# Turning two adjacency tiles per late neighbour product in a graph attention and GraphSAGE kernel

## The chip, the cores and the metric

The kernel runs on one core of a Trainium2 chip. The metric is the device time of one execution in microseconds (us); lower is better. The timed runs shown are three, and one more execution was profiled.

## The reference

16 graphs (the batch) of 1024 nodes with 512 features each and a dense 0/1 adjacency matrix go through two layers. Each layer is followed by a residual and a layer norm over the features:

```python
feats = einsum('bnf,hfu->bhnu', X, W)                    # 8 heads x 64 units
dense = leaky_relu(e_self[..., :, None] + e_neigh[..., None, :], 0.2)
att = softmax(dense + NEG_BIG * (1.0 - A), axis=-1)
x1 = layernorm(x + relu(concat_heads(att @ feats) + b))  # layer 0

agg = (adj @ x1) / max(adj.sum(-1), 1e-6)                # layer 1
out = layernorm(x1 + relu(concat([x1, agg]) @ W1.T))
```

## The kernel before

**Tiles.** A graph's 1024 rows are T = 8 row tiles of 128, and HALF is 4. The adjacency matrix of a graph is loaded in the same 8 row tiles of 512 KB in f32. Each is transposed on TensorE (`turn_adj`: 8 transposes of 128x128 on the bf16 halves of the words into one PSUM bank) and evicted by VectorE into `adj_t` (`adj_rows`: times a constant, written as uint16). The whole `adj_t` of a batch is used by the masks of all 8 heads, by the degree and by the aggregation of layer 1, so it can be overwritten for the next batch only when the aggregation is done.

**Slots and banks.** The raw adjacency tiles have three slots in `adj_nat` (`ADJ_SLOTS`): tile t goes to slot t % 3 and can be loaded when tile t - 3 has been turned. Turned tiles alternate between PSUM banks 3 and 7 (`ADJ_BANKS`), so the turn of tile t waits for the eviction of tile t - 2. Tiles 0 and 1 share their slots with the first four row tiles of the next batch (`lead_x`), tile 2 has its slot to itself. The tiles from 3 on are loaded late, by `load_late_adj`, which first waits for the turn that frees the slot.

**A batch.** On each engine the order of the work is written out by hand in a function `batch(b, more)`; it stands in a hardware loop over batches 0 to 14 and once more, written out, for batch 15. The engines meet only at semaphores. Within a batch TensorE does, in this order: the head (score product of the second half of the rows, features of row tiles 4 and 5, turns of adjacency tiles 6 and 7, features 6 and 7); 8 heads of 8 masked key tiles each (48 small matmuls a key tile); the degree; scores and features of the first half of the next batch; the aggregation; and the tail. The tail loops over row tiles t = 0 to 7: neighbour product, own product of t + 1, turn of x1 tile t + 2. In its second half it also holds turns for the next batch: `turn_adj(b + 1, t - HALF)` and `turn_x(b + 1, t)`. Behind the loop stand the turns of tiles 4 and 5 and two waits for the last row tile's results:

```python
                if more:
                    turn_adj(b + 1, 4)
                    turn_adj(b + 1, 5)
                    pe.wait_ge(o2_sb.sem, o2_sb.at(b, T))
                    pe.wait_ge(o_sum.sem, o_sum.at(b, T))
```

**The other engines in the tail.** For each row tile t ScalarE divides the neighbour product by the degree (`by_degree`, L422 through L414). VectorE's `ln1(t)` adds the two products (L779), adds the residual (L783) and takes the statistics (L786, L789); `ln1_end(t)` normalises (L794, L797) into `y_out`, which has two halves, so that tile t waits until the store of tile t - 2 has landed (`y_stored`). `ln1_end(t - 1)` follows `ln1(t)`. Ahead of the sum, from t = 5 on, `ln1` holds the split of a row tile of the next batch (`x_low`, L600) and one `adj_rows` (L605). In the next batch's head, VectorE's `adj_rows(b, 6)` stands ahead of the values of the first head and `adj_rows(b, 7)` behind them.

**SyncE's queue.** All loads and stores are issued by SyncE from one queue in the order written, with its waits in between. In the tail each t holds: a wait for the residual of tile t, the row load of tile t for the next batch, the store of t - 2, and from t = 4 on one late adjacency load. At the start of a batch's heads it stores the scores, loads the first two score broadcasts, and waits for the turns of tiles 6 and 7 before it loads the leading row tiles of the next batch.

**The prologue** ahead of the loop does for batch 0 what the tail does for the others, with tiles 0 to 5 turned and evicted.

Of the kernel before, what the change touches and what calls it, by code (L numbers as in the profile page):

```python
# [43 lines left out]
def gat_sage_kernel(nc, x, adj, gat_w, gat_b, gat_self, gat_neigh, sage_w, out):  # L44
    B, N, D = x.shape
    H, _, U = gat_w.shape
    T = N // P
    KC = D // P
    HALF = T // 2
# [21 lines left out]
    with ExitStack() as ctx:  # L71
# [180 lines left out]
        def rows(v):  # L252

            return v.rearrange("h u -> (h u)").partition_broadcast(P)
# [4 lines left out]
        def col(c):  # L259
            return slice(c * P, (c + 1) * P)  # L260
# [4 lines left out]
        def stand(engine):  # L265

            engine.sem_inc(turnstile, 1)
# [3 lines left out]
        @block.sync  # L271
        def _(sp):
            for c in range(KC):
                sp.dma_start(w_raw[:, c, :].rearrange("p (h u) -> p h u", h=H),
                             gat_w[:, col(c), :].rearrange("h p u -> p h u")).then_inc(w_in[0], 16)
            for t in range(HALF):
                sp.dma_start(lead_x[:, t, :], x[0, t * P:(t + 1) * P, :]).then_inc(lead_in[t].sem, 16)
            sp.dma_start(a_bc[:, 0, :], rows(gat_self)).then_inc(w_in[1], 16)
            sp.dma_start(a_bc[:, 1, :], rows(gat_neigh)).then_inc(w_in[1], 16)
            sp.dma_start(bias_bc[:, :], rows(gat_b)).then_inc(w_in[2], 16)  # L280
            sp.dma_start(sage_raw, sage_w.rearrange("(c p) f -> p c f", p=P)).then_inc(w_in[3], 16)
            sp.sem_inc(y_stored[0], 16)
            sp.sem_inc(y_stored[1], 16)

            def load_x(b, t):
                sp.dma_start(xs[:, t, :], x[b, t * P:(t + 1) * P, :]).then_inc(x_in[t].sem, 16)

            def load_lead(b, t):
                sp.dma_start(lead_x[:, t, :], x[b, t * P:(t + 1) * P, :]).then_inc(lead_in[t].sem, 16)

            def load_tail(b, t):
                sp.dma_start(tail_x[:, t - HALF, :], x[b, t * P:(t + 1) * P, :]).then_inc(tail_in[t - HALF].sem, 16)

            def load_adj(b, t):
                s = t % ADJ_SLOTS
                sp.dma_start(adj_nat[:, s, :], adj[b, t * P:(t + 1) * P, :]).then_inc(a_in[s].sem, 16)

            def load_late_adj(b, t):
                sp.wait_ge(at_ps.sem, at_ps.at(b, t - ADJ_SLOTS + 1))
                load_adj(b, t)  # L300

            def store_y(b, t):
                sp.wait_ge(y_ok.sem, y_ok.at(b, t + 1))
                sp.dma_start(out[b, t * P:(t + 1) * P, :], y_out[:, t % 2, :]).then_inc(y_stored[t % 2], 16)

            def store_scores(b, i):
                sp.wait_ge(sc_f32.sem, sc_f32.at(b, i + 1))
                half = slice(i * HALF * P, (i + 1) * HALF * P)
                sp.dma_start(s_dram[:, half], sc_row[0:H, half]).then_inc(s_stored.sem, 16)

            def load_scores(b, h):
                if h >= 2:
                    sp.wait_ge(stepped.sem, stepped.at(b, (h - 1) * T))
                sp.dma_start(s_bc[:, h % 2], s_dram[h].partition_broadcast(P)).then_inc(s_in[h % 2].sem, 16)

            def first_scores(b):

                store_scores(b, 1)
                sp.wait_ge(s_stored.sem, s_stored.at(b, 32))
                load_scores(b, 0)  # L320
                load_scores(b, 1)

            load_adj(0, 2)
            for t in range(HALF, T):
                load_tail(0, t)
            sp.wait_ge(w1_ps, 2 * KC)
            for t in range(T):
                load_x(0, t)
            for s in range(2):
                sp.wait_ge(xt_ps.sem, xt_ps.at(0, 2 * s + 2))  # L330
                load_adj(0, s)
            store_scores(0, 0)
            for t in range(3, T):
                load_late_adj(0, t)
            with sp.Fori(0, B - 1) as b:
                first_scores(b)
                for s in range(2):
                    sp.wait_ge(at_ps.sem, at_ps.at(b, T - 1 + s))
                    stand(sp)
                    load_lead(b + 1, 2 * s)  # L340
                    load_lead(b + 1, 2 * s + 1)
                load_adj(b + 1, 2)
                for h in range(2, H):
                    load_scores(b, h)
                    if h in (3, 4):
                        s = h - 3
                        sp.wait_ge(xt_ps.sem, xt_ps.at(b + 1, 2 * s + 2))
                        stand(sp)
                        load_adj(b + 1, s)
                sp.wait_ge(masked.sem, masked.at(b, H * T))  # L350
                stand(sp)
                for t in range(HALF, T):
                    load_tail(b + 1, t)
                store_scores(b + 1, 0)
                for t in range(T):
                    sp.wait_ge(res_ok.sem, res_ok.at(b, t + 1))
                    load_x(b + 1, t)
                    if t >= 2:
                        store_y(b, t - 2)
                    if t >= 4:  # L360
                        load_late_adj(b + 1, t - 1)
                store_y(b, T - 2)
                store_y(b, T - 1)
                load_late_adj(b + 1, T - 1)
            first_scores(B - 1)
            for h in range(2, H):
                load_scores(B - 1, h)
            for t in range(T):
                store_y(B - 1, t)
            for s in range(2):  # L370
                sp.wait_ge(y_stored[s], 16 * (B * T // 2 + 1))
# [161 lines left out]
        def _(dve):  # L533
# [87 lines left out]
            def batch(b, more):  # L621
# [26 lines left out]
                dve.wait_ge(chain.sem, chain.at(b, steps[0]))  # L648
                dve.tensor_scalar(ts_hi[:], ts[:], 0.0, None, ALU.max).then_inc(weights_in.sem, 1)
                feature_rows(b, 5)  # L650
                adj_rows(b, 6)
                for s in range(2):
                    dve.wait_ge(y_stored[s], b * (16 * T // 2) + 16)
                dve.wait_ge(ft_sb.sem, ft_sb.at(b, HALF))
                dve.wait_ge(weights.sem, weights.at(b, 2))
                dve.wait_ge(ones_ok.sem, ones_ok.at(b, 1))
                value_parts(b, 0, FIRST)
                adj_rows(b, 7)
                dve.wait_ge(at_sb.sem, at_sb.at(b, T))


# [106 lines left out]
                def ln1(t):  # L768

                    s = t % 2  # L770
                    if t >= 2:
                        dve.wait_ge(y_ok.sem, y_ok.at(b, t - 1))
                    if more and t == T - 1:
                        ones_column(b + 1)
                    if more and t >= HALF + 1:
                        x_low(b + 1, t - 1)
                        adj_rows(b + 1, t - HALF - 1)
                    dve.wait_ge(o2_sb.sem, o2_sb.at(b, t + 1))
                    dve.tensor_tensor(z[:, s], bank[O1_BANKS[s]][:], o2s[:, s], ALU.add).then_inc(o_sum.sem, 1)  # L779
                    if more and t == T - 1:  # L780
                        x_low(b + 1, T - 1)
                    dve.wait_ge(o_sum.sem, o_sum.at(b, t + 1))
                    dve.scalar_tensor_tensor(out=z[:, s], in0=z[:, s], scalar=0.0, in1=xs[:, t, :],  # L783
                                             op0=ALU.max, op1=ALU.add).then_inc(res_ok.sem, 1)
                    dve.wait_ge(res_ok.sem, res_ok.at(b, t + 1))
                    dve.bn_stats(stats[:, s], z[:, s]).then_inc(chain.sem, tick())  # L786
                    dve.wait_ge(chain.sem, chain.at(b, steps[0]))
                    stand(dve)
                    dve.bn_aggr(mv1[:, s], stats[:, s]).then_inc(ln1_mv.sem, 1)  # L789
# [25 lines left out]
                    if t >= 1:  # L815
                        ln1_end(t - 1)
                if more:
                    adj_rows(b + 1, 3)
                ln1_end(T - 1)
                if more:  # L820
                    adj_rows(b + 1, 4)
                    adj_rows(b + 1, 5)
                assert steps[0] == chain.per_batch, steps

            dve.wait_ge(w_in[2], 16)
# [5 lines left out]
            first_maximum(0)  # L831
            for t in range(HALF, T):
                x_low(0, t)
            for t in range(6):
                adj_rows(0, t)
            with dve.Fori(0, B - 1) as b:
                batch(b, True)
# [3 lines left out]
        def _(pe):  # L841
# [59 lines left out]
            def batch(b, more):  # L901
# [9 lines left out]
                pe.wait_ge(diag_ok.sem, diag_ok.at(b, 1))  # L911
                mm(bank[6][:, 0:SC], ones16[:], diag16[:], True, True).then_inc(max_ps.sem, 1)
                features(b, 5)
                turn_adj(b, 6)
                turn_adj(b, 7)

                def key_tile(h, jt, queries):

# [119 lines left out]
                for t in range(T):  # L1038
# [8 lines left out]
                        own(t + 1)  # L1047
                    if t + 2 < T:
                        turn_x1(t + 2)
                    if more and t >= HALF:  # L1050
                        turn_adj(b + 1, t - HALF)
                    if more and HALF <= t < T - 1:
                        turn_x(b + 1, t)
                    if more and t == T - 2:
                        turn_x(b + 1, T - 1)
                if more:
                    turn_adj(b + 1, 4)
                    turn_adj(b + 1, 5)
                    pe.wait_ge(o2_sb.sem, o2_sb.at(b, T))
                    pe.wait_ge(o_sum.sem, o_sum.at(b, T))  # L1060

# [5 lines left out]
            pe.wait_ge(ft_sb.sem, ft_sb.at(0, 2))  # L1067
            for t in range(HALF, T):
                turn_x(0, t)
            for t in range(6):  # L1070
                turn_adj(0, t)
            with pe.Fori(0, B - 1) as b:
                batch(b, True)
# [23 lines left out]
```

## Time and profile before

| | |
|---|---|
| median of 3 runs | 3609.08 us (3599.88 to 3612.85) |
| profiled execution | 3602.66 us, span 3600.9 us |
| granted TensorE clock, mean | 0.974 |
| TensorE busy | 3413.5 us, 95% of the span |
| VectorE busy | 2467.0 us, 69% |
| ScalarE busy | 1738.2 us, 48% |
| GpSimd busy | 285.0 us, 8% |
| DMA | 248.58 MB, mean 69 GB/s |

The span runs from the first to the last instruction of the program. PE is TensorE, DVE is VectorE, ACT is ScalarE, SP is SyncE. A batch takes about 222 us; the first batch boundary is at about 277 to 300 us of the span. Matmuls overlap, so a duration is longer than the distance to the next start.

### The profile page before, as it was taken

Reading aid. Unit: us, or ns where it says so; the run is one execution under the profiler, and the core shown is the slowest. Engines: PE = TensorE matmul, PEld = TensorE weight load, DVE = VectorE, ACT = ScalarE, POOL = GpSimd, SP = SyncE. Lnnn points to the kernel's source line nnn. Section 1 sums busy time; section 2 is a strip of 40 time slices with the busy share of each in tenths; the row PEclk is TensorE's granted clock in tenths of the full one; section 3 lists DMA queues with packets and bytes.
Section 4 is the critical chain, followed back from the end, with each engine's and each line's share of the span. In section 5 each row is a group of like instructions: output and inputs, shape, how many; then the busy total and the mean of one; then the engine's idle time right before and its main releaser. Section 6 shows DMA issues by size and latency. Waiting matters only on the chain.

```text
span 3600.9 us, 136785 instructions
## 1 busy us (share of the span) xinstructions
PE 3413.5 (95%) x59456; PEld 2912.9 (81%) x59456; DVE 2467.0 (69%) x4364; ACT 1738.2 (48%) x2185; POOL 285.0 (8%) x253
## 2 busy tenths in 40 slices
PE   6998989989899998999989899898998989989998
PEld 5978879787796877969779697886977869788795
DVE  5857668576685756858578485774857758576685
ACT  2635436364363644626346273462735527355363
POOL 0010100101001010100101001010010100101001
PEclk9999999999999999999999999999999999999999
DMA  5113031120312203122031220312203131130310
GB/s 170 59 38 108 26 113 57 51 99 23 116 51 60 96 18 122 45 76 81 20 125 39 77 79 25 125 33 89 68 27 123 33 98 59 38 118 27 94 33 24
DMA packets 98408, 248.58 MB, mean 69 GB/s; under 512 B 14720, under 2 KB 14720, under 8 KB 97792
## 3 DMA queue, kind: packets, MB, share of 16 engines
q1 hardware_dynamic: 97792, 239.38, 20.6%
q8 instruction: 507, 8.31, 1.0%
q14 instruction: 109, 0.89, 0.1%
HBM read 205.26 MB, written 34.08 MB: 66 GB/s over the span
## 4 chain that ended last, share of the span: by engine, by line
PE 94%; issue 3%; DVE 2%; ACT 1%; DMA 0%; SPq 0%; POOL 0%; ACTq 0%; DVEq 0%; POOLq 0%
PE six L843 77%; PE pair L843 12%; PE six L988 2%; PE pair L872 1%; PE pair L881 1%; PE six L872 1%; PE six L881 1%; DVE trl L600 0%; DVE stats L786 0%; ACT mask L414 0%; DVE adj_t L605 0%; DVE s_bc L783 0%; PE six L909 0%; DVE mask L797 0%; DVE mask L544 0%
## 5 line engine op out<-in xcount | busy, mean ns | idle before, releaser
L843 PE MATMUL six<-x_parts,mask 128*128 128x65 bf16 x16384 | 1550.7, 193 | 1.0 <-issue 0.9
L843 PE MATMUL six<-third,mask 128*128 128x65 bf16 x16384 | 1550.4, 193 | 0.6 <-issue 0.2
L843 PE MATMUL six<-rest,mask 128*128 128x65 bf16 x16384 | 1550.6, 194 | 0.0
L843 PEld LDWEIGHTS six<-x_parts,mask 128*128 128x128 fp8e4 x16384 | 1537.5, 97 | 5.7 <-issue 4.9
L843 PEld LDWEIGHTS six<-third,mask 128*128 128x128 fp8e4 x16384 | 1536.4, 97 | 0.6 <-issue 0.6
L843 PEld LDWEIGHTS six<-rest,mask 128*128 128x128 fp8e4 x16384 | 1533.9, 97 | 3.2 <-issue 1.4
L441 ACT ACTIVATE step<-s_bc,n_step 128x1024 uint16<-128x1024 f32 x1024 | 1094.2, 1138 | 382.8 <-DVE mask L671 382.0
L671 DVE TENSOR_TENSOR mask<-adj_t,step 128x1024 uint16<-128x1024 uint16 x1024 | 651.3, 685 | 24.5 <-ACT step L441 22.6
L843 PE MATMUL six<-adj_t,x_parts 128*128 128x512 fp8e4 x1536 | 388.5, 380 | 2.7 <-ACT x_parts L463 1.5
L392 POOL TENSOR_TENSOR s_bc<-feat,rden 128x512 f32<-128x512 f32 x112 | 124.0, 1112 | 3071.8 <-DVE s_bc L714 3043.0
L843 PEld LDWEIGHTS six<-adj_t,x_parts 128*128 128x128 f16 x1536 | 146.4, 98 | 179.3 <-issue 18.3
L414 ACT ACTIVATE mask<-six,rdeg 128x512 f32<-128x512 f32 x128 | 88.2, 689 | 343.6 <-PE six L843 343.6
L414 ACT ACTIVATE trh<-six 128x512 fp32r<-128x512 f32 x160 | 88.5, 601 | 270.9 <-PE six L843 213.8
L843 PE MATMUL six<-w1h,trh 128*128 128x512 f32 x512 | 214.6, 419 | 0.0
L589 DVE TENSOR_TENSOR x_parts<-six,qry_w 128x130 f32<-128x130 f32 (+2 forms) x272 | 111.0, 408 | 143.9 <-PE six L843 143.4
L843 PE MATMUL six<-w0h,trh 128*128 128x512 f32 x512 | 205.1, 401 | 0.0
L803 DVE TENSOR_TENSOR trl<-six,trh 128x512 fp32r<-128x512 f32 x96 | 60.2, 683 | 211.0 <-ACT trh L414 211.0
L843 PE MATMUL six<-w0h,trl 128*128 128x512 f32 x512 | 202.0, 394 | 0.0
L843 PE MATMUL six<-w0l,trh 128*128 128x512 f32 x512 | 201.9, 394 | 0.0
L843 PE MATMUL six<-w1l,trh 128*128 128x512 f32 x512 | 200.2, 391 | 0.0
L843 PE MATMUL six<-w1h,trl 128*128 128x512 f32 x512 | 200.0, 391 | 0.0
L463 ACT ACTIVATE x_parts<-xs,nb,rs 128x512 f16<-128x512 f32 x128 | 104.2, 814 | 150.8 <-DVE nb L736 150.8
(118 smaller groups left out, 4830.5 us busy)
## 6 DMA issues: line engine op xcount, KB each, us to landing
adj_nat<-in_adj_dram SPq DMA_DIRECT2D x128, 512.0 KB, 4.7
s_bc<-self_scores SPq DMA_DIRECT2D x128, 512.0 KB, 3.7
xs<-in_x_dram SPq DMA_DIRECT2D x128, 256.0 KB, 2.8
out_dram<-mask SPq DMA_DIRECT2D x128, 256.0 KB, 3.0
adj_nat<-in_x_dram SPq DMA_DIRECT2D x64, 256.0 KB, 3.4
step<-in_x_dram SPq DMA_DIRECT2D x64, 256.0 KB, 3.5
xs<-in_L_gnn_W_dram SPq DMA_DIRECT2D x1, 2048.0 KB, 11.9
feat<-in_L_gnn_W_dram SPq DMA_DIRECT2D x4, 256.0 KB, 4.3
```

Source lines behind the costliest of these rows:

```text
L392: pool.tensor_tensor(z[:, t % 2].rearrange("p (h u) -> p h u", h=H), feat[:, t, :, 0:U], rden[:, t, :].unsqueeze(2).broadcast_to([P, H, U] ...
L414: return act.activation(o, i, ACT.Copy, scale=scale)
L441: act.activation(step[:, g % STEP_SLOTS], s_bc[:, h % 2], ACT.Sigmoid, scale=STEP, bias=n_step[:, jt, h:h + 1]).then_inc(stepped.sem, 1)
L463: act.activation(x1h[:, t, :], xs[:, t, :], ACT.Identity, bias=nb[:, t:t + 1], scale=rs[:, t:t + 1]).then_inc(x1_hi.sem, 1)
L589: dve.tensor_tensor(scaled, sums[:, :, :, 1, :], factor, ALU.mult).then_inc(lower_ok.sem, k1 - k0)
L671: dve.tensor_tensor(mask[:, g % MASK_SLOTS], adj_t[:, jt, :], step[:, g % STEP_SLOTS], ALU.logical_shift_left).then_inc(masked.sem, 1)
L803: dve.tensor_tensor(trl[:, f, :], bank[AGG_BANKS[half][f]][:], trh[:, f, :].bitcast(F32), ALU.subtract).then_inc(aggt_lo.sem, 1)
L843: return pe.matmul(o, l, r, start=start, stop=stop, skip_group_check=True)
L872: ins = pe.transpose(bank[XT_BANKS[t]][:, col(k)], source[:, col(k)], ident[:])
L881: ins = pe.transpose(bank[ADJ_BANKS[t % 2]][:].bitcast(BF16)[:, col(jt)], adj_halves[t % ADJ_SLOTS][:, col(jt)], ident_bf[:])
L988: ins = pe.transpose(bank[5][:, col(k)], xs[:, t, col(k)], ident[:])
```

## The change

TensorE turns two adjacency tiles each at t = 4, 5 and 6 of the tail (0 to 5), and tiles 6 and 7 behind the loop; the head has none. VectorE evicts two tiles each ahead of the sums of row tiles 5, 6 and 7, and tiles 6 and 7 ahead of the last normalisation. SyncE issues the late loads ahead of the wait for the residual, the row load and the store: tiles 3 and 4 at t = 4, 5 and 6 at t = 5, tile 7 at t = 6. The prologue turns and evicts all eight tiles of batch 0.

```diff
@@ sync, tail of a batch
                 for t in range(T):
+                    for late in {4: (3, 4), 5: (5, 6), 6: (7,)}.get(t, ()):
+                        load_late_adj(b + 1, late)
                     sp.wait_ge(res_ok.sem, res_ok.at(b, t + 1))
                     load_x(b + 1, t)
                     if t >= 2:
                         store_y(b, t - 2)
-                    if t >= 4:
-                        load_late_adj(b + 1, t - 1)
                 store_y(b, T - 2)
                 store_y(b, T - 1)
-                load_late_adj(b + 1, T - 1)
@@ vector, head of a batch
                 feature_rows(b, 5)
-                adj_rows(b, 6)
...
                 value_parts(b, 0, FIRST)
-                adj_rows(b, 7)
                 dve.wait_ge(at_sb.sem, at_sb.at(b, T))
@@ vector, ln1(t)
                     if more and t >= HALF + 1:
                         x_low(b + 1, t - 1)
-                        adj_rows(b + 1, t - HALF - 1)
+                        adj_rows(b + 1, 2 * (t - HALF - 1))
+                        adj_rows(b + 1, 2 * (t - HALF - 1) + 1)
@@ vector, end of the tail
                 if more:
-                    adj_rows(b + 1, 3)
+                    adj_rows(b + 1, 6)
+                    adj_rows(b + 1, 7)
                 ln1_end(T - 1)
-                if more:
-                    adj_rows(b + 1, 4)
-                    adj_rows(b + 1, 5)
@@ vector, prologue
-            for t in range(6):
+            for t in range(T):
                 adj_rows(0, t)
@@ tensor, head of a batch
                 features(b, 5)
-                turn_adj(b, 6)
-                turn_adj(b, 7)
@@ tensor, tail
-                    if more and t >= HALF:
-                        turn_adj(b + 1, t - HALF)
+                    if more and HALF <= t < T - 1:
+                        turn_adj(b + 1, 2 * (t - HALF))
+                        turn_adj(b + 1, 2 * (t - HALF) + 1)
                     if more and HALF <= t < T - 1:
                         turn_x(b + 1, t)
                     if more and t == T - 2:
                         turn_x(b + 1, T - 1)
                 if more:
-                    turn_adj(b + 1, 4)
-                    turn_adj(b + 1, 5)
+                    turn_adj(b + 1, 6)
+                    turn_adj(b + 1, 7)
                     pe.wait_ge(o2_sb.sem, o2_sb.at(b, T))
                     pe.wait_ge(o_sum.sem, o_sum.at(b, T))
@@ tensor, prologue
-            for t in range(6):
+            for t in range(T):
                 turn_adj(0, t)
```

## Rows read from the trace of the kernel before

**Rows 1.** The page, part 1: busy time, share of the span and instructions.
```profile
PE 3413.5 (95%) x59456; PEld 2912.9 (81%) x59456; DVE 2467.0 (69%) x4364; ACT 1738.2 (48%) x2185; POOL 285.0 (8%) x253
```

**Rows 2.** All waits, whole span: who, for what, us in total, times, longest.
```profile
PE pair L881 <- DVE adj_t L605: 71.1, 15, 4.7
PE pair L843 <- issue: 69.5, 14, 6.3
```

**Rows 3.** Timeline of PE, 1613 to 1620: start, us, instruction, [idle before].
```profile
1618.64 0.79 PE L843 MATMUL pair<-trh,wah_wide 128*128 128x512 f32 x1 [3.96 <-issue]
```

**Rows 4.** The chain that ended last, 140 to 460: start, us, what.
```profile
278.60 0.06 DVE s_bc L779
...
279.21 0.68 DVE trl L600
...
282.10 0.70 DVE adj_t L605
...
282.93 1.01 PE pair L881 x8
283.94 4.71 issue
...
300.33 0.45 PE pair L881 x8
```

**Rows 5.** Timeline of PE, 240 to 302.
```profile
266.68 0.61 PE L881 MATMUL pair<-ident_bf,adj_nat 128*128 128x128 bf16 x8
...
277.12 0.62 PE L881 MATMUL pair<-ident_bf,adj_nat 128*128 128x128 bf16 x8
```

**Rows 6.** Timeline of PE, 3387 to 3396, the last boundary.
```profile
3393.16 0.78 PE L843 MATMUL pair<-trh,wah_wide 128*128 128x512 f32 x1
```

**Rows 7.** Timeline of DVE, 240 to 302.
```profile
264.44 0.69 DVE L779 TENSOR_TENSOR s_bc<-pair,mask 128x512 f32<-128x512 f32 x1 [0.76 <-ACT mask L414]
...
273.79 0.55 DVE L797 TENSOR_SCALAR mask<-s_bc,mv,rs 128x512 f32<-128x512 f32 x1
...
278.60 0.69 DVE L779 TENSOR_TENSOR s_bc<-pair,mask 128x512 f32<-128x512 f32 x1 [2.55 <-ACT mask L414]
...
293.95 0.68 DVE L631 TENSOR_REDUCE nmax<-sc_row 16x1 f32<-16x512 f32 x1 [8.18 <-ACT sc_row L414]
```

**Rows 8.** By tile: `adj_nat` and `out_dram` 281 to 286, `s_bc` 295 to 296.3.
```profile
DMA to landing us min/median/max: 5.8/5.9/6.0
...
DMA to landing us min/median/max: 2.9/4.9/6.2
...
DMA to landing us min/median/max: 3.9/4.4/4.8
```

**Rows 9.** Timeline of SP, 258 to 270: when DMAs are issued.
```profile
265.89 0.33 SPq L286 DMA_DIRECT2D xs<-in_x_dram  x1
266.42 0.36 SPq L304 DMA_DIRECT2D out_dram<-mask  x1
```

**Rows 10.** Timeline of PE, 64 to 68, the end of the prologue.
```profile
65.68 1.04 PE L881 MATMUL pair<-ident_bf,adj_nat 128*128 128x128 bf16 x8 [0.63 <-DMA adj_nat<-in_adj_dram]
66.47 0.78 PE L843 MATMUL pair<-trh,wah_wide 128*128 128x512 f32 x1
```

**Rows 11.** By tile: `adj_nat` on SP, 65 to 65.5, the load of tile 7.
```profile
L296 SPq DMA_DIRECT2D adj_nat<-in_adj_dram x1: 328/328/328, 65.1 to 65.1; - x1
...
DMA to landing us min/median/max: 4.3/4.3/4.3
```

**Rows 12.** Windows: stretch, us, busy (x) PE, PEld, DVE, ACT, POOL, clock, DMA, GB/s.
```profile
281.90:288.60 6.70, 1.01 (x8) 0.78 (x8) 2.70 (x6) 1.28 (x1) 0.00 (x0) 0.50 0.94 299
288.60:292.10 3.50, 3.44 (x8) 2.78 (x9) 0.00 (x0) 0.00 (x0) 0.00 (x0) 0.50 0.08 30
```

**Rows 13.** Timeline of ACT, 299 to 302.
```profile
300.77 2.19 ACT L441 ACTIVATE step<-s_bc,n_step 128x1024 uint16<-128x1024 f32 x2
```

**Rows 14.** Timeline of PE, 306 to 306.4: the first masked product.
```profile
306.26 0.20 PE L843 MATMUL six<-x_parts,mask 128*128 128x65 bf16 x1
```

## The prediction

> **What bounds the kernel now.** I read the page first: TensorE is busy for 95% of the span [rows 1], so only what shortens its work or its idle time can show. Then the list of all waits: of TensorE's own idle time two entries make 140 us of the 187 that are left, namely 15 waits of 4.7 us for an adjacency eviction on VectorE and 14 pauses of 4.0 to 6.3 us, mean 69.5 / 14 = 4.96, that end without a semaphore [rows 2, 3]. Then the chain that ended last, around the first batch boundary, to see where the two stand [rows 4]. TensorE's last neighbour product is over at 277.1, and it turns tiles 3 and 4 [rows 5]. The turn of tile 5 waits for the eviction of tile 3, and that one stands in VectorE's order behind the whole of the last row tile: the division by degree on ScalarE, the sum at 278.60, the split of x, the residual, the statistics and the normalisation of tile 6. It starts at 282.10, the turn at 282.93, and then comes the pause of 4.71 [rows 4]. I take the pause for the jump back of the loop: it is there at 14 boundaries and missing at the fifteenth, where the last batch is written out behind the loop and the first score product has no idle time ahead of it [rows 6].
>
> From the score product on TensorE is not idle for long until the next boundary. So the boundary is the stretch to price, and after it the two turns in the next batch's head.
>
> **What the change does, part by part.** All times are those of the boundary at 277, and every step is taken 15 times.
>
> *Turns.* Eight turns a batch before and after, 0.45 each at full clock [rows 4]. Before, three stand ahead of the last neighbour product, three behind it, two in the head behind feature tile 5. Afterwards six stand ahead (two each at t = 4, 5, 6) and two behind. Ahead of the last product that costs 3 x 0.45 = 1.35; in the head it saves 0.9.
>
> *The wait.* Tiles 6 and 7 need the evictions of tiles 4 and 5, which now stand on VectorE ahead of the last sum. What TensorE waits for last is now the sum itself (the waits at the end of the loop). That was done by about 279.2, when VectorE went on to the next instruction [rows 4]; with the 1.35 it is 280.55. The two turns fit in between: from 277.1 + 1.35 = 278.45 on, 0.9 of work.
>
> *The pause.* It stays. From the last turn's end (283.94) it is 4.96 in the mean; from that turn's release (282.93) it is about 5.97. Behind a bare wait it can be either, since the sequencer may have run to the jump before the last transposes ended. I take the first and 0.25 more, because transposes leave the sequencer shortly before their modelled end. New start of the scores: 280.55 + 4.96 + 0.25 = 285.76; old: 283.94 + 4.96 = 288.90. Gain 3.14, with bounds of 2.38 (280.55 + 5.97) and 3.39 (no addition). The Trainium skill says that a taken branch out of the sequencer's window forces a fetch of the target page by DMA (Runtime: NRT & Kernel Launch, Instruction fetch mechanics); by that rule the pause could also change with what the DMA engines carry meanwhile. Nothing in the sum hangs on it.
>
> *Per boundary* 3.14 + 0.9 = 4.04 (3.3 to 4.3), x 15 = 60.6 (49 to 64).
>
> *VectorE.* One more eviction ahead of each of row tiles 5, 6 and 7, at most 0.7 each by the one in the chain [rows 4]. Ahead of row tile 5 it was idle 0.76 and the degree division comes 0.45 later, ahead of 7 it was idle 2.55 [rows 7], so they are hidden; without that cover each would cost its 0.7. Behind the last sum it has tiles 6 and 7 where it had 3, 4 and 5. At the boundary it stood idle for 8.18 until the next batch's scores. These now come 3.1 earlier, and its last eviction ends about when it did. If VectorE too pauses at its jump, for no more than the 6.3 that TensorE shows, it is back in time or 0.5 late, and TensorE has a feature product (2.8) before it needs the maximum: nothing.
>
> *Loads and stores (SyncE's queue).* The loads of late tiles 3 and 4 now stand ahead of the row load and the store of t = 4, tiles 5 and 6 ahead of those of t = 5, tile 7 ahead of t = 6. Tile 3: issued 260.6, needed at 267.6. Tile 5: its slot is free when tile 2 is turned, 266.68 + 0.9 = 267.6 [rows 5]; needed at 274.4, so 6.8 us. Tile 7: its slot is free at about 274.4, issued 274.6, needed from 279 and harmless until 280.1, so 5.5 us. Of the two late loads around a boundary, with most queued around them, the landings took 5.8 and 6.0 [rows 8]. So tiles 3 and 5 are in time; tile 7 may be up to 0.5 late. Queued behind these are the row loads, which nothing wants until the next batch's norm, and the stores, which the normalisation waits for. The store of t = 5 goes out at 267.6 + 0.45 + about 1.2 (two loads and a row load at 0.5 each) = 269.2 instead of 266.42 [rows 9]; VectorE wants it landed at 273.79 + 0.9 = 274.7 [rows 7], so 5.5 us. Stores took 2.9 to 6.2 [rows 8]: VectorE stalls for 0 to 0.7, out of 2.3 of slack (2.55, plus 1.35 less 0.9 of shift, less 0.7 of eviction). I take nothing.
>
> *Prologue.* Tiles 6 and 7 of batch 0 were turned in the head, under other work. Now TensorE waits ahead of the loop: tile 7's load is issued at 65.1 and takes 4.3, so 69.4, then a turn of 0.79 at the lower clock (65.68 to 66.47), and the scores start at 70.2 instead of 66.47 [rows 10, 11]. Cost 3.7 less 0.9: 2.8 once.
>
> *Clock.* TensorE's granted clock is 0.50 (1.2 of 2.4 GHz) from 281.9 to 292.1, and the first 3.5 us of scores run at it [rows 12]. New idle stretch: from about 279.5 to 285.8, 6.3 us. The old stretch ahead of the turn was 4.74 and the clock had gone by its end, so I expect it to go again, and 3.5 us at half speed, 1.75 us, are lost as before: no term. At the fifteenth boundary, without a jump, only 1 us of idleness stays and some 2 us may come back once.
>
> **Sum.** 60.6 - 2.8 = 57.8 us. From the profiled execution's 3602.66 that is 3544.9. The runs shown have their median 6.4 above it; taken from 3609.08 it is 3551.3. I forecast 3548, between the two, and count the rivals from there (no change is 3606 on that scale). A measurement of this kernel tells about 0.5%, 18 us, from no change, so the forecast is well outside.
>
> **The rivals.**
>
> *A, part of it goes to VectorE's and ScalarE's inputs: 3571.* The four lead row loads and one adjacency load of the next batch waited for the turns in the head (300); these are now past, so the loads follow directly on the two score broadcasts, whose landings took 3.9 and 4.8 [rows 8]. If they share the engines instead of queueing, 2.5 MB at the 299 GB/s of the crowded stretch [rows 12] are 8.4 us, and the first broadcast lands about 4 us later. The first step tile starts at 300.77 and the first masked product at 306.26 [rows 13, 14]; 304.8 + 1.1 for the step + 0.7 for the mask = 306.6 against 306.26 - 0.9 = 305.36, so 1.3 to 1.7 us a batch are lost, about 25 us. Against it: the first of the two broadcasts lands as fast as a load that has nothing behind it (tile 7's in the prologue took 4.3 [rows 11]), so what follows in the queue does not seem to slow it. The Trainium skill says that descriptors of one ring are consumed in ring order but a later one may finish its write earlier (DMA: Bandwidth & Descriptors, Queues, rings and completion order); no landing here shows this. A late tile 7 or the 5.97 pause gives the same size.
>
> *B, the clock stays up: 3522.* If the single stretch of idleness does not lower the clock, 1.75 us a boundary come back, 26 in all. For it: one stretch where two stood close together. Against it: 4.74 was enough before.
>
> *C, no change: 3595.* The pause may not be the jump but something that ends at a fixed time, such as VectorE reaching its next batch; then the scores still start near 288.7, and the 0.9 of the head is all that is gained, less the prologue: 15 x 0.9 - 2.8 = 10.7 us. The fifteenth boundary speaks against it.
>
> *D, slower: 3632.* The store of t = 5, and with it those of 4 and 6, lands behind two adjacency loads and a row load. Each us of landing beyond 7.8 (5.5 + 2.3) pushes the last sum and so the boundary; at 7.8 + 57.8 / 15 = 11.7 the whole gain is eaten, and at 13.4 the kernel is 1.7 x 15 = 26 us slower. The longest landing shown is 6.2.
>
> **How the numbers follow.** Forecast 0.60, A 0.16, B 0.12, C 0.07, D 0.05. The range reaches past B (3515) and past A (3580); beyond it lie C, D and the far end of B, some 0.17. Faster than by 0.5%: the forecast, A and B, 0.88. Same: C, 0.07. Slower: D, 0.05.
>
> **What would show it.** In the profile after: no 4.7 us wait of the adjacency turn for an adjacency eviction; the pause of 4 to 6 us still 14 times, now behind a wait of about 1 us for the sum; 0.50 clock at the boundary as before; a batch 4 us shorter; in the head no turns; the stores of t = 4, 5 issued 1.6 to 3 us later and VectorE's waits for them still short. Wrong would be: waits of TensorE for adjacency loads in the tail (tiles 3, 5, 7), VectorE idle ahead of the normalisation of tiles 4 and 5 by more than 2 us, ScalarE's first step tile late, or scores that start no earlier.

## The result, and the profile after

The changed kernel takes 3542.68 us in the median of 4 runs (3538.92 to 3545.30), the kernel before 3604.48 in the same comparison. The ratio is 0.9826, with a 95% interval of 0.9801 to 0.9851. It was profiled in an execution of 3544.41 us, against 3602.66 before: 58.25 us less, where the sum of the prediction gave 57.8. By the medians it is 61.8 less.

The page of the changed kernel, its head and part 1, answers to [rows 1]:

```profile
span 3542.6 us, 136785 instructions
...
PE 3416.6 (96%) x59456; PEld 2916.5 (82%) x59456; DVE 2462.9 (70%) x4364; ACT 1735.7 (49%) x2185; POOL 285.2 (8%) x253
```

The same instructions do the same work; what shrank is TensorE's idle time, from 187 to 126 us. The list of all waits of the changed kernel answers to [rows 2]:

```profile
PE pair L839 <- issue: 71.5, 14, 5.5
...
DVE mask L795 <- DMA out_dram<-mask: 42.8, 30, 2.2
...
PE pair L877 <- DMA adj_nat<-in_adj_dram: 3.1, 3, 1.6
...
PE six L877 <- DVE adj_t L604: 1.8, 3, 1.2
```

The 15 waits of 4.7 us for an eviction are gone. The waits for adjacency loads that are left all stand ahead of the loop, in the prologue, and none in a tail. The 14 pauses ahead of the scores are still there, with the same total (71.5, was 69.5), but this total now contains the wait for the sum, as the chain shows. VectorE's waits for a store have doubled in number (19.1 us in 15 before). This is the chain that ended last in the changed kernel at the first boundary (start, us, what), to be laid beside [rows 4]:

```profile
281.78 0.69 ACT mask L413
...
282.50 0.05 DVE s_bc L777
...
283.10 0.69 DVE trl L599
283.80 3.33 issue
287.12 5.11 PE pair L839 x12
292.23 2.79 PE six L839 x12
```

Before, residual, statistics, normalisation, eviction and a turn of 1.01 stood between the split of x and the pause. Now the chain goes from the split straight into the pause. The timeline of TensorE, 250 to 300, shows the turns where the change puts them, without an idle mark, and the scores behind them (compare [rows 5]):

```profile
276.48 0.62 PE L877 MATMUL six<-ident_bf,adj_nat 128*128 128x128 bf16 x8
276.93 0.61 PE L877 MATMUL pair<-ident_bf,adj_nat 128*128 128x128 bf16 x8
...
281.01 0.62 PE L877 MATMUL six<-ident_bf,adj_nat 128*128 128x128 bf16 x8
281.47 0.61 PE L877 MATMUL pair<-ident_bf,adj_nat 128*128 128x128 bf16 x8
287.12 0.79 PE L839 MATMUL pair<-trh,wah_wide 128*128 128x512 f32 x1 [5.04 <-issue]
```

The batch can be cut into stretches by the starts of TensorE's matmuls: the last neighbour product, the first score product, the first and the last masked product. I read these starts from the timeline of every batch. Means over the 14 boundaries with a jump (the tail and the masked products over the 15 batches of the loop), in us:

```
                                          before   after   difference
last neighbour product to first score      12.19    6.78    -5.41
tail (last aggregation product to last     40.66   42.00    +1.34
  neighbour product)
head (first score to first masked)         17.99   17.31    -0.68
masked products (first to last)            98.51   98.98    +0.47
```

With the fifteenth boundary (7.04 to 3.37), a start of the loop that is 3.8 later and 1.4 less in the first head, these add up: -79.4 at the boundaries, +20.1 in the tails, -12.6 in the stretches called head, of all 16 batches, +9.9 in the masked products and what follows them, +3.8 in the prologue, together -58.2.

### The profile page after: what moved, and what is told of

The parts are those of the page before. It is cut to its first block, busy times and chain, and to the rows that moved or that the text cites. A ratio compares the mean times of both kernels' runs of the same rounds, so it can differ in the third digit from the quotient of the medians.

```text
span 3542.6 us, 136785 instructions
## 1 busy us (share of the span) xinstructions
PE 3416.6 (96%) x59456; PEld 2916.5 (82%) x59456; DVE 2462.9 (70%) x4364; ACT 1735.7 (49%) x2185; POOL 285.2 (8%) x253
## 4 chain that ended last, share of the span: by engine, by line
PE 95%; issue 2%; DVE 1%; ACT 1%; DMA 0%; SPq 0%; POOL 0%; ACTq 0%; DVEq 0%; POOLq 0%
PE six L839 78%; PE pair L839 12%; PE six L982 2%; PE pair L868 1%; PE six L868 1%; PE six L877 1%; PE pair L877 1%; DVE trl L599 0%; ACT mask L413 0%; PE six L905 0%; DMA adj_nat<-in_adj_dram 0%; DVE mask L543 0%; DVE wa L545 0%; DVE xs L718 0%; DMA s_bc<-in_L_gnn_a_neigh_dram 0%
## 5 line engine op out<-in xcount | busy, mean ns | idle before, releaser
L413 ACT ACTIVATE x1t_h<-six 128x512 fp32r<-128x512 f32 x128 | 77.0, 601 | 208.0 <-PE six L982 208.0
```

The source lines that it names most:

```text
L413: return act.activation(o, i, ACT.Copy, scale=scale)
```

## Experiments

Each ran in five timed rounds, save one that was only profiled. Ratios are to the kernel before on the same chip; the pair in brackets is the 95% interval.

**Only the one late tile.** The kernel before, with tile 5 turned in the head.

```diff
                 if more:
                     turn_adj(b + 1, 4)
-                    turn_adj(b + 1, 5)
...
                 features(b, 5)
+                turn_adj(b, 5)
                 turn_adj(b, 6)
                 turn_adj(b, 7)
```

VectorE's `adj_rows` of tile 5 moves the same way, and the prologue ends at tile 4.

> The kernel before with one edit: tile 5 is turned and evicted in the head of the next batch, not behind the tail's loop; nothing else moves. Theory W (the gain is that TensorE no longer waits for an eviction behind the norm; how many tiles are turned per product is worth nothing): the stretch from the last neighbour product to the scores falls from 12.2 us to about 6.7 as in the changed kernel, the tail stays at 40.7 (the change made it 42.0), the head grows by 0.45 to 18.4 (the change made it 17.3): a batch as long as the changed kernel's within 0.3 us, no prologue cost, so about 3540 us, ratio to before 0.982. Theory H (turning early and emptying the head is what pays): it keeps less than half of the gain, above 3570.

3549.06 us, ratio 0.9828 (0.9814 to 0.9842). The stretch to the scores is 6.72 and the tail 40.66, both as theory W has them, but the head is 19.15, not 18.4, and the median is 9 us above the 3540 of that theory. The waits of this kernel say why, and its timeline of TensorE shows one of them:

```profile
PE pair L881 <- DVE adj_t L605: 9.0, 16, 0.6
```

```profile
513.00 0.61 PE L881 MATMUL pair<-ident_bf,adj_nat 128*128 128x128 bf16 x8 [0.56 <-DVE adj_t L605]
```

With three turns in a row in the head, tile 7 waits for the eviction of tile 5. So one tile in another place gives 59.2 of the 70.0 us by which the medians of the changed kernel and of the kernel before differ on the same chip, and the two ratios (0.9828 and 0.9805) have intervals that overlap. Of the 10.8 us between the two medians, the stretches of the two profiles other than the masked products explain 4; a wait of 0.56 in each head is 9.0 in all, and the shorter prologue gives 5 back.

**Tile 7 behind feature tile 6.** As above, with one more move.

```diff
                 turn_adj(b, 6)
-                turn_adj(b, 7)
                 features(b, 6)
+                turn_adj(b, 7)
                 features(b, 7)
```

> The kernel before with tile 5 turned in the head, and tile 7 turned behind feature tile 6, not ahead of it. In the kernel with tile 5 in the head and tile 7 right behind tile 6, TensorE waited 0.56 us for the eviction of tile 5 ahead of the turn of tile 7 in each head. If that wait is the whole of what that kernel lacked against the changed one, the head falls from 19.15 to 18.5 us and the ratio to before from 0.983 to 0.980 or 0.981, that of the changed kernel. If turning two tiles per product is worth something by itself, it stays at 0.983.

3538.48 us, ratio 0.9819 (0.9805 to 0.9832). The 0.56 us waits are gone from the list and the head is 18.67; the ratio lies between the two that I expected, and its interval reaches both. Against the changed kernel profiled on the same chip the tail is 1.34 shorter and the head 1.4 longer, so a batch is as long outside its masked products; the prologue is 6.1 shorter, and longer masked products in that one execution (99.13 a batch against 98.73) took those 6 us back. To turn two tiles per product is worth nothing that these runs can tell.

**The loads behind the rows.** The changed kernel with the late loads behind the row load and the store of the same t.

```diff
-                    for late in {4: (3, 4), 5: (5, 6), 6: (7,)}.get(t, ()):
-                        load_late_adj(b + 1, late)
                     sp.wait_ge(res_ok.sem, res_ok.at(b, t + 1))
                     load_x(b + 1, t)
                     if t >= 2:
                         store_y(b, t - 2)
+                    for late in {4: (3, 4), 5: (5, 6), 6: (7,)}.get(t, ()):
+                        load_late_adj(b + 1, late)
```

> The changed kernel with the late adjacency loads behind the row load and the store of the same row tile, at the same t. Theory 1 (the queue order is worth nothing, all of it is hidden): VectorE's 1.3 us wait for the store ahead of the normalisation of row tile 5 goes away, the load of tile 5 goes out about as before since it waits for its turn anyway, and the time stays within 0.3% of the changed kernel's 3543. Theory 2 (the loads had to be in front): tile 5's or tile 7's load is late by 1 us or more, TensorE waits for it, and it costs 1 us x 15 or more, above 3558.

3542.67 us, ratio 0.9813 (0.9797 to 0.9830), against 0.9805 (0.9791 to 0.9819) of the changed kernel on the same chip: no difference. Its waits:

```profile
DVE mask L795 <- DMA out_dram<-mask: 19.8, 15, 1.8
PE pair L877 <- DMA adj_nat<-in_adj_dram: 7.7, 17, 1.4
```

VectorE's extra stall for a store is gone (42.8 to 19.8 us) and bought nothing; TensorE waits a little more for adjacency tiles, 7.7 us in 17 waits, mostly for tile 7, where it would wait for the sum anyway. Theory 1 holds.

**More data around the jump.** The changed kernel with four stores to spare memory.

```diff
                     if t >= 2:
                         store_y(b, t - 2)
+                    if t == T - 2:
+                        sp.wait_ge(o2_ps.sem, o2_ps.at(b, T))
+                        sp.wait_ge(extra, b * 64 + 64)
+                        for k in range(4):
+                            sp.dma_start(spare[k], w1h[:, k, :].bitcast(F32)).then_inc(extra, 16)
```

> The changed kernel with four stores of 256 KB from constant weights to spare memory, issued when the last neighbour product is done, so that 1 MB more moves around the jump. It tells why the pause after the wait for the sum is 4.2 us (from the start of the split of x behind the sum to the first score product) where I had taken 5.2. Theory T (data in the DMA engines holds up the fetch of instructions; before, 1.0 to 1.4 MB moved in the 4.5 us ahead of the scores, after the change 0.5): the 4.2 grow to 5 or more and the kernel is 12 us or more slower. Theory R (in the old kernel the pause was long because the transposes of tile 5 at half clock stood ahead of the jump): it stays at 4.2 within 0.3 and the time within 0.3%.

3545.32 us, ratio 0.9826 (0.9812 to 0.9839). From the start of the split to the first score the mean is 4.70, against 4.17 in the changed kernel profiled on the same chip; the DMA engines moved 1.2 MB in the last 4.5 us of it, as in the kernel before, and not 0.5. The first boundary, in this kernel's timelines of VectorE and TensorE:

```profile
282.89 0.68 DVE L608 TENSOR_TENSOR trl<-six,trh 128x512 fp32r<-128x512 f32 x1
```

```profile
287.51 0.79 PE L848 MATMUL pair<-trh,wah_wide 128*128 128x512 f32 x1 [5.64 <-issue]
```

So theory T is right in direction and too large by half: data costs the pause 0.53 us, 7 us over 14 boundaries. The two medians (3545.3 and 3538.2) differ by as much, but their intervals overlap and the medians alone would not show it; the pause does. What the pause of the kernel before had beyond that is left to theory R: 5.97 from its last release, less 4.70, is 1.27, of which the turn of tile 5 at half clock is 1.01. The other 0.26 belongs to that one execution. In the second profile of the kernel before (below) the pauses are

```profile
PE pair L843 <- issue: 65.8, 14, 7.1
```

and 65.8 / 14 = 4.70 behind the turn is the 4.70 that this kernel has behind a bare wait.

**The changed kernel again, and the kernel before again**, both unedited.

> The changed kernel once more, unedited. The heads of a batch (from the first to the last masked product) took 98.5 us in the mean before and 99.0 after the change, 8 us over 16 batches, in small gaps of 0.2 to 0.6 us that no semaphore ends. Theory N (chance of one execution): in this profile the heads take another value between 98.1 and 99.1. Theory S (a cost of the change): 99.0 again within 0.1, and the kernel before, profiled elsewhere, stays at 98.5.

> The kernel before, unedited, for its profile. The heads of a batch took 98.5 us in the mean in its one profile and 98.7 to 99.2 in those of the changed kernel and its variants. Theory N (the small fetch gaps of the heads are chance): 98.3 to 99.2 here too. Theory S (the change lengthens the heads): 98.5 within 0.1.

The changed kernel again takes 3538.21 us, ratio 0.9805 (0.9791 to 0.9819). The masked products of a batch take 98.73 us in this profile (98.98 in the first) and 98.69 in the second profile of the kernel before (98.51 in the first); over the variants they go from 98.39 to 99.34. Of the 0.47 us a batch between the first two profiles, 0.04 are left between the second two, so theory N holds for most of it; 0.2 us a batch as a cost of the change can't be excluded by four profiles. The repeat also shows how the other stretches scatter: the stretch to the scores is 0.36 shorter in the second profile of the kernel before than in the first, and its head 0.35 longer. The gain is 62 us in one set of runs and 70 in the other.

**TensorE's loop with two batches per pass.** The changed kernel.

```diff
-            with pe.Fori(0, B - 1) as b:
-                batch(b, True)
+            with pe.Fori(0, B // 2 - 1) as i:
+                batch(i * 2, True)
+                batch(i * 2 + 1, True)
+            batch(B - 2, True)
             batch(B - 1, False)
```

> The changed kernel with TensorE's loop alone holding two batches per pass (7 passes, batches 14 and 15 behind it), so that 8 of the 14 jumps of TensorE are gone and the other engines jump as before. Theory J (the pause is TensorE's jump): the stretch from the last neighbour product to the scores is 3.4 us at 9 boundaries and 6.7 at 6. What follows depends on VectorE: its last normalisation ends at about 289.2 at the first boundary, and if it pauses 4 us at its own jump, TensorE then waits 3 to 5 us for the maximum in the head and next to nothing is gained, 3535 to 3543. If VectorE's jump is free, 8 x 3.4 plus the clock, which stays up there, are gained: about 3505. Theory C (the pause is something else that ends at a fixed time): the stretch stays at 6.7 everywhere.

3518.81 us, ratio 0.9761 (0.9748 to 0.9774). The stretch to the scores is 3.3 us at the 9 boundaries without a jump and 6.6 to 7.1 at the 6 with one, one after the other, so the pause is TensorE's jump and theory C falls. The time lies between the two that I gave for VectorE: TensorE waits for the maximum in the head, as the list of waits says, 8 times for 15.3 us in all, up to 2.0:

```profile
PE pair L839 <- DVE diag L633: 15.3, 8, 2.0
```

VectorE, which still jumps there, shows a pause of its own of 2.4 to 2.8 us that no semaphore ends, ahead of its reading of the new scores:

```profile
DVE nmax L630 <- issue: 20.3, 8, 2.7
```

**All four engines with two batches per pass.** The same edit on VectorE, ScalarE and SyncE.

> As the kernel with two batches per pass of TensorE's loop, but with two per pass on VectorE, ScalarE and SyncE too. Theory J: at 9 boundaries no engine jumps, TensorE's stretch is 3.4 us instead of 6.7 and its clock stays at 1.00, the head takes 16.5 instead of 17.3: 8 x (3.4 + 0.8) = 33 us less than the changed kernel, about 3507, unless VectorE's last normalisation, which waits for a store, is still late for the next maximum; then 8 x 2 = 16 less, 3524. Theory C: no gain.

3498.60 us, ratio 0.9707 (0.9694 to 0.9720), 8 us below what I expected, since the head also is 15.0 to 15.8 us after a boundary without a jump. Two boundaries of its timeline of TensorE, one without a jump and one with:

```profile
282.44 0.61 PE L885 MATMUL pair<-ident_bf,adj_nat 128*128 128x128 bf16 x8
284.81 0.50 PE L847 MATMUL pair<-trh,wah_wide 128*128 128x512 f32 x1 [1.76 <-DVE trl L605]
...
502.99 0.79 PE L847 MATMUL pair<-trh,wah_wide 128*128 128x512 f32 x1 [5.35 <-issue]
```

And its windows around both (stretch, us, busy time of PE, PEld, DVE, ACT, POOL, granted clock, DMA share, GB/s):

```profile
281.00:300.00 19.00, 17.24 (x92) 13.43 (x90) 11.95 (x27) 7.01 (x12) 0.00 (x0) 1.00 0.64 207
500.00:515.00 15.00, 12.01 (x48) 9.53 (x49) 5.86 (x18) 3.26 (x7) 0.00 (x0) 0.77 0.44 152
```

Without the jump TensorE is idle for 1.76 us, the granted clock stays at 1.00, and the first score product starts 0.7 us after the start of the split of x (4.3 at the boundary at 500). VectorE's pause is gone too where its loop doesn't jump: there it goes from its last normalisation to the scores with no idle time, so that pause is VectorE's own jump.

**No waits at the end of the tail.** The changed kernel.

```diff
                     turn_adj(b + 1, 7)
-                    pe.wait_ge(o2_sb.sem, o2_sb.at(b, T))
-                    pe.wait_ge(o_sum.sem, o_sum.at(b, T))
```

> The changed kernel without TensorE's two waits at the end of the tail (for the division and the sum of row tile 7); the score product behind the jump waits for the split of x, which stands behind that sum on VectorE. Theory J with a jump that starts when the last turn is issued: TensorE's pause now runs beside the wait for the sum, the stretch falls from 6.7 to about 5.7, and 14 x 1.0 = 14 us are gained, about 3526. If the jump only starts when the split is done, or the fetch waits for something else, nothing changes (3540).

3523.70 us, ratio 0.9771 (0.9758 to 0.9785). The stretch to the scores falls to 4.8, by 1.9 and not 1.0: from the last turn's end it is 3.37 (2.8 to 3.6 at the 14 boundaries) where a pause from a release is 3.9 to 4.5, so the jump seems to begin before the last turn is over, beside the wait. The packet that brings the loop's first instructions (next section) points the same way: in the changed kernel it begins 1.3 to 1.9 us behind the start of the split of x, here 0.5 us in the mean behind the last turn's end. But the head grows to 18.7, since VectorE is now the late one. So the time came out near the expected 3526 by two misses against each other, 27 us gained at the boundaries where 14 were expected and 19 lost in the heads where none was. TensorE's timeline at one boundary and the waits:

```profile
502.19 0.49 PE L839 MATMUL pair<-trh,wah_wide 128*128 128x512 f32 x1 [3.37 <-issue]
```

```profile
PE pair L839 <- DVE diag L633: 18.3, 11, 3.1
```

And VectorE's timeline at the boundary with one of the longest of them:

```profile
2233.84 0.55 DVE L795 TENSOR_SCALAR mask<-s_bc,mv,rs 128x512 f32<-128x512 f32 x1 [2.90 <-DMA out_dram<-mask]
2237.06 0.67 DVE L630 TENSOR_REDUCE nmax<-sc_row 16x1 f32<-16x512 f32 x1 [2.67 <-issue]
```

VectorE waits 2.90 for a store ahead of its last normalisation, and then makes its pause at the jump, 2.67.

**Both.** Two batches per pass on all four engines, and no waits at the end of the tail.

> Both at once on top of the changed kernel: two batches per pass on TensorE, VectorE, ScalarE and SyncE, and no waits of TensorE at the end of the tail. At the 6 boundaries that keep a jump the stretch falls from 6.8 to about 4.8 as in the kernel without the end waits, 12 us; there the head then grew by 1.4 us a batch in the mean because TensorE waited in it, which would take back up to 6 x 1.4 = 8. Expected 3487 to 3495 on the scale where the two-batch kernel has 3499, so the fastest of all.

3493.20 us, ratio 0.9686 (0.9672 to 0.9701), within the range expected: the lowest time, 3.1% below the kernel before and 1.2% below the changed one by the ratios 0.9686 and 0.9805. Its interval still touches that of the kernel with the waits (0.9694 to 0.9720), so these runs don't tell the two apart with certainty. The stretch at the boundaries with a jump is 4.2 to 5.2, the head after them 17.7 to 19.5.

## Why the prediction was right, point by point

*The wait.* Right. TensorE now waits for the sum of the last row tile alone. That sum starts 1.48 us after the first turn behind the last product before (277.12 to 278.60) and 1.49 after the change (281.01 to 282.50), and both turns fit in.

*The pause.* It stayed, 14 times, and it is the jump: the kernels with two batches per pass show it at every second boundary. Its size was the one term that I mis-sized. I took 5.21 from the sum on (4.96 plus 0.25); the chain shows 283.10 to 287.12, 4.02, and the mean is 4.2. So the stretch fell by 5.41 where I had 3.14 + 1.35 = 4.49, which is 0.9 a boundary, 13 us. I had measured the pause beside 1.2 MB of transfers, where 0.5 MB are left after the change; that is 0.53 by the run with extra stores. Of the rest, 0.26 is chance, the 4.96 of one execution against 4.70 in the next, and the 0.25 that I added was not needed: from the turn's end before, and from a bare wait beside the same transfers, the pause is 4.70 alike. The three come to 1.0, as near to 0.9 as the executions agree. Between the two second profiles the stretch fell by 5.1. The fetch itself can be seen in the transfers of the changed kernel between 284.2 and 285.2: 

```profile
q8 instruction: 1, 0.02, 6.6%
```

One packet of 16 KB, 2.7 us ahead of the scores; there is one 2.6 to 3.0 us ahead of them at all 14 boundaries with a jump in this profile and in that of before, and none at the fifteenth. With two batches per pass on all engines it is there at the 6 boundaries with a jump (2.6 to 3.2 us ahead), and within 6 us of the scores at none of the others. That the target's page has to be fetched by DMA after a taken branch is what the Trainium skill states (Runtime: NRT & Kernel Launch, Instruction fetch mechanics), and these packets agree. The same section of the Trainium skill names such stalls as a reason to unroll; two batches per pass gave 1.0% (0.9707 against 0.9805).

*Turns.* 1.35 more in the tail: 1.34. 0.9 less in the head: 0.68 between the first two profiles, where the lower clock lasts 0.6 us longer into the scores after the change, and 1.07 between the second two, where it lasts 0.2 less. So the term was right as far as two executions agree.

*VectorE.* The added evictions were hidden: ahead of the last sum it still stood idle for 1.47. The store of t = 5 went out at 272.73 and landed 5.6 later; VectorE stalled 1.27 for it, where I had 0 to 0.7 out of 2.3. In its timeline:

```profile
278.47 0.55 DVE L795 TENSOR_SCALAR mask<-s_bc,mv,rs 128x512 f32<-128x512 f32 x1 [1.27 <-DMA out_dram<-mask]
...
282.50 0.69 DVE L777 TENSOR_TENSOR s_bc<-pair,mask 128x512 f32<-128x512 f32 x1 [1.47 <-ACT mask L413]
...
292.89 0.67 DVE L630 TENSOR_REDUCE nmax<-sc_row 16x1 f32<-16x512 f32 x1 [3.71 <-ACT sc_row L413]
```

The store went out 1.0 later than my step had it (269.2, plus 2.5 by which this tail starts later, is 271.7), for two reasons: three issues at 0.5 are 1.5 and not the 1.2 of my sum, and the two loads of that t took 1.57 together, where two others, at t = 4, took 0.85. SyncE's timeline:

```profile
270.45 1.57 SPq L296 DMA_DIRECT2D adj_nat<-in_adj_dram  x2
...
272.73 0.35 SPq L304 DMA_DIRECT2D out_dram<-mask  x1
```

That this stall costs nothing is shown by the kernel with the loads behind the rows, where it is gone and the time is the same. VectorE's own jump, for which I allowed up to 6.3, is 2.4 to 2.8 where it can be seen. Here it lies within the idle stretch of 3.7, and it showed only when the end waits or TensorE's jumps were taken away.

*Prologue.* 70.28 for the start of the scores against 70.2 forecast, and 1.4 less in the first head where I had 0.9 (compare [rows 10]):

```profile
69.49 1.04 PE L877 MATMUL pair<-ident_bf,adj_nat 128*128 128x128 bf16 x8 [0.88 <-DMA adj_nat<-in_adj_dram]
70.28 0.78 PE L839 MATMUL pair<-trh,wah_wide 128*128 128x512 f32 x1
```

*Clock.* It fell again at each boundary with a jump, as forecast. The windows of the changed kernel answer to [rows 12]:

```profile
283.80:287.10 3.30, 0.00 (x0) 0.00 (x0) 3.08 (x7) 1.50 (x2) 0.00 (x0) 0.65 0.47 146
287.10:291.60 4.50, 4.48 (x11) 3.52 (x12) 0.79 (x3) 0.07 (x1) 0.00 (x0) 0.50 0.37 137
```

It falls while TensorE pauses and is back at 291.65, so 4.5 us of scores run at half speed here and not 3.5. Over the 14 boundaries it is 4.3 and 5.1 in the two profiles of before, 5.0 and 4.8 in those after: taking no term for it was right. At the fifteenth boundary, where 1.85 us of idleness stay and no pause, I had expected it to stay up. It fell for 3.4 us just behind the start of the scores, in this profile and in its repeat, and did not fall in the profiles of the kernels with the loads behind the rows, with the extra stores and with tile 7 later. The idleness ahead of it was 1.85 us both with the fall and, in the last two of these, without, so it doesn't decide it alone, and what does stays open.

*The rivals.* A: the lead loads do follow directly on the two score broadcasts (issued at 295.53, they waited for the turns at 300.59 before), and ScalarE's first step tile starts at 299.74, 12.6 after the first score; before it was 300.77 less 288.65, 12.1. Half a microsecond and not 4, and no wait of TensorE behind it. (Its own sum was a little off: 306.6 less 305.36 is 1.2 a batch, not 1.3 to 1.7.) B and C fell by the clock and by the boundaries without a jump. D: the store landed 1.3 late, not 6.

*The sum.* 60.6 at 15 boundaries was forecast. Measured, without the masked products, it is 79.4 - 20.1 + 11.2 = 70.5, and between the second two profiles 74.9 - 20.1 + 15.9 = 70.7. The masked products of the first pair of executions, and what follows them, took 9.9 us back, most of it chance by the second pair. So the 58.25 against 57.8 is luck: the batches' gain outside the masked products was forecast 10 us too small, by the pause, and 10 us went the other way. The changed kernel's second set of runs, 70 us below before, is nearer to what its boundaries show.

## What to carry to other kernels

Ask of a wait on the path not how to speed up what it waits for, but what stands ahead of it in the other engine's written order: here an eviction of 0.7 us stood behind a whole layer norm, and moving one tile brought most of the change (0.9828 against 0.9805). Before a pause at a loop's end is carried to another place, take it from more than one execution and check what ran beside it: 4.96 in one profile was 4.70 in the next, and 4.17 with less data moving. Where every engine jumps at the same time, the jumps hide each other; take them away from all engines at once, and let the last wait of a loop body run beside the jump.

## What the runs showed of the hardware

With a jump of TensorE's loop it takes 3.9 to 4.5 us from the start of the split of x, behind the last wait, to the first matmul, 0.7 without; the stretch to the scores is 6.8 with it and 3.3 without, and it holds one 16 KB instruction packet, 2.6 to 3.0 us ahead of that matmul. The jump costs 0.5 us more with 1.2 MB of transfers beside it. VectorE pauses too (2.4 to 2.8 us at its jumps, none where its loop doesn't jump). Without the end waits the pause from the last turn's end is 2.8 to 3.6, so TensorE's jump seems to begin while transposes are still running. In the kernel with two batches per pass on all engines the 1.76 us of idleness that stay at a boundary without a jump left the clock at 2.4 GHz, which gave the next head another 1 to 2 us. The mean granted clock of that kernel is 0.993, against 0.974 before.
